# Two or four heads of a narrow causal tile in one PSUM bank: one exponential, one maximum and one mask product for them all

## The reference: one transformer block with modulation, causal attention and routed experts

```python
h = _layernorm(x) * (1 + ca) + sa
scores = jnp.einsum('bnqd,bnkd->bnqk', q, k) * HEAD_DIM ** (-0.5)
scores = jnp.where(causal, -jnp.inf, scores)          # causal: key after query
attn = jax.nn.softmax(scores, axis=-1)
out = jnp.einsum('bnqk,bnkd->bnqd', attn, v)
x = x + ga * (out @ W_out.T + b_out)
h = _layernorm(x) * (1 + cb) + sb
x = x + gb * ffn(h)      # top-4 of 16 experts per token, in 2 of 4 groups, and a shared one
```

## Time and profile before

| | |
|---|---|
| median of 3 runs | 617.59 us (617.16 to 618.82) |
| the profiled execution, its own time | 618.35 us |
| its span, first to last instruction | 616.6 us, mean granted TensorE clock 0.98 |
| busy PE, DVE, ACT, POOL | 93%, 77%, 60%, 55% of the span |
| passes 0 to 6, start to start | 32.5, 31.9, 31.8, 31.7, 37.9, 40.5, 39.6 us |
| pass 7 until its last score | 34.7 us |
| of that: exponentials L1470 | 384, 165.6 us busy |
| maxima L1586 | 384, 193.8 us busy |
| mask products L2159 | 256, 54.2 us busy |

### The profile page before, as it was taken

One profiled execution on the slowest core, in us unless ns is written; L12 is line 12 of the kernel. 1 busy time (PEld: TensorE's weight loads), 2 busy tenths in 40 slices (PEclk: granted clock), 3 DMA queues, 4 the chain that ended last, 5 costly groups with the idle time before them and its releaser, 6 DMA issues. The chain is left out here.

```text
span 616.6 us, 13827 instructions
## 1 busy us (share of the span) xinstructions
PE 570.7 (93%) x4003; PEld 386.2 (63%) x4003; DVE 472.2 (77%) x1404; ACT 372.6 (60%) x877; POOL 340.4 (55%) x646
## 2 busy tenths in 40 slices
PE   8997899999999999998987988989999999999985
PEld 7885533434343444444342466778799999999971
DVE  5868988889888769777958468898977677677647
ACT  4764566667666556655858553454566666666650
POOL 6015562656567455854648786774155655555560
PEclk9989999999999999999989879999999999999997
DMA  8489579874438281751215133567994444444895
GB/s 293 113 198 265 154 151 213 215 183 98 156 85 239 95 197 77 178 187 51 107 44 182 72 134 127 189 229 216 387 390 134 132 141 131 135 140 132 304 318 209
DMA packets 65891, 107.96 MB, mean 175 GB/s; under 512 B 13705, under 2 KB 52377, under 8 KB 64026
## 3 DMA queue, kind: packets, MB, share of 16 engines
q1 hardware_dynamic: 58954, 87.93, 49.7%
q0 software_dynamic: 6864, 19.15, 8.0%
HBM read 60.90 MB, written 43.88 MB: 170 GB/s over the span
## 5 line engine op out<-in xcount | busy, mean ns | idle before, releaser
L1470 ACT ACTIVATE Pr<-bank 128x512 f32<-128x512 f32 (+3 forms) x384 | 165.6, 495 | 97.5 <-PE bank L2276 93.5
L1586 DVE TENSOR_REDUCE mxA<-bank 128x1 f32<-128x128 f32 (+3 forms) x256 | 112.1, 483 | 20.1 <-PE bank L2161 19.7
L2276 PE MATMUL bank<-Qs,Ks 99*128 99x512 bf16 (+3 forms) x384 | 118.7, 334 | 5.0 <-ACT Pr L1470 3.2
L2161 PE MATMUL bank<-Ks,Qs 96*128 96x512 bf16 (+3 forms) x384 | 119.0, 327 | 1.2 <-DVE mxB L1586 0.6
L1292 POOL DMA_INDIRECT expert_rows<-Y,YIX x79 | 77.2, 977 | 74.2 <-ACT Y L1533 71.7
L1586 DVE TENSOR_REDUCE mxB<-bank 128x1 f32<-128x512 f32 x128 | 81.7, 681 | 13.5 <-PE bank L2161 13.5
L2262 PE MATMUL bank<-Pr,Vst 128*32 128x512 f32 (+3 forms) x768 | 83.1, 506 | 3.0 <-POOL Pr L1271 3.0
L1269 POOL TENSOR_TENSOR tick<-ident 128x1 f32<-128x1 f32 x128 | 25.3, 198 | 106.1 <-ACT Pr L1470 105.3
L2526 PE MATMUL bank<-W,xh 128*128 x316 | 78.1, 328 | 1.0 <-issue 1.0
L1221 POOL DMA_INDIRECT chosen_rows<-Hx,pos x64 | 67.2, 1049 | 20.4 <-issue 18.6
L2276 PEld LDWEIGHTS bank<-Qs,Ks 99*128 99x128 bf16 x384 | 35.9, 98 | 58.9 <-ACT Pr L1470 39.2
(11 more groups left out here) (256 smaller groups left out, 1263.6 us busy)
## 6 DMA issues: line engine op xcount, KB each, us to landing
G<-chosen_rows SPq DMA_DIRECT2D x79, 134.0 KB, 2.6
W<-expert_words SPq DMA_DIRECT2D x7, 1088.0 KB, 7.6
qk_parts<-AP SPq DMA_DIRECT2D x32, 192.0 KB, 3.1
Z<-expert_rows SPq DMA_DIRECT2D x12, 512.0 KB, 6.3
Wraw<-in_wexp SPq DMA_DIRECT2D x9, 608.0 KB, 6.4
SA<-in_wexp SPq DMA_DIRECT2D x7, 608.0 KB, 4.5
Vst<-Vall SPq DMA_DIRECT2D x8, 512.0 KB, 5.7
expert_words<-SH SPq DMA_DIRECT2D x7, 480.0 KB, 2.8
```

Of the source, the lines that this page charges most:

```text
L1470: nc.scalar.activation(Pr[(2 * s + j // 2) % 4][:, j % 2, 0:w], ebank[p % RING][:, 0:w], ACT.Exp, scale=SCALE).then_inc(exp_done, EXP)
L1586: nc.vector.tensor_reduce(dst, mbank[u % RING][:, 0:w], AX.X, ALU.max).then_inc(m_red, 1)
L2161: nc.tensor.matmul(mbank[u % RING][:, 0:w], Qs[slot][0:NPR, i // TPC, j, (i % TPC) * P:(i % TPC + 1) * P], Ks[slot][0:NPR, j, k0:k0 + w], ...
L2276: nc.tensor.matmul(ebank[p % RING][:, 0:CH - q0], Ks[slot][0:NAUG, j, kt * P:(kt + 1) * P], Qs[slot][0:NAUG, qc, j, q0:CH], start=True, st ...
```

## The change: groups instead of heads

A score tile, or unit, of width w no longer stands for one head but for n = min(4, 512 // w) heads that lie side by side in one bank: one head at 512 and 384 columns, two at 256, four at 128. Both lists (`UNIT_GROUPS`, `HEAD_GROUPS`) shrink from 48 to 38 entries a pass. A group has one exponential with an output of n rows in `Pr`, one maximum with n outputs, and one mask product whose moving operand repeats the 128 mask columns n times; its score matmuls stay one per head, and only the last of them signals. POOL's masks stay as they were, two heads at a time, but both pairs of a 128-wide step now wait for the same exponential. The rings still have three banks; the bank index now runs on over the passes, since 38 is no multiple of 3. `interleave()` places the new entries by the same rule with summed widths; the lead-in gets new counts of units per place; `UNIT_DVE` is renumbered by hand to the shorter list, and in pass 6 two routing steps follow some units. A piece of ACT's that stood after a step's second exponential now stands after the group that holds head 1.

```diff
+def packed(widths):
+    groups = []
+    for i, w in enumerate(widths):
+        n = min(HG, CH // w)
+        groups += [(i, j, n) for j in range(0, HG, n)]
+    return groups
+UNIT_GROUPS = packed([w for _, _, _, w in ROWS])
+HEAD_GROUPS = packed([step_width(_s) for _s in range(NS)])
+UNITS, HEADS = len(UNIT_GROUPS), len(HEAD_GROUPS)
...
-    unit_cost = [w + 200 for _, _, _, w in ROWS for _ in range(HG)]
-    head_cost = [CH - max(0, kt - TPC * qc) * P + EXTRA for qc, kt in STEPS for _ in range(HG)]
+    unit_cost = [n * ROWS[r][3] + 200 for r, _, n in UNIT_GROUPS]
+    head_cost = [n * step_width(i) + EXTRA for i, _, n in HEAD_GROUPS]
...
-PER_V2, PER_QK3, PER_V3 = 4, 3, 2
+PER_QK3 = 3
+AT_V2 = (0, 3, 6, 9, DIAG_UNITS)
+AT_V3 = tuple(DIAG_UNITS + 4 * KH * PER_QK3 + i for i in (0, 1, 2, 3, 3))
...
-    **{(5, 41 + t): [("aggr", 1, t)] for t in range(TPC)}, (6, 1): [("soft", 0)],
-    **{(6, 5 + i): [("route", 0, 1 + i, 2 + i)] for i in range(23)},
+UNIT_DVE.update({(6, 4): [("soft", 0)], (6, 29): [("route", 0, PLACED, PLACED + 1)], (6, 31): [("route", 0, PLACED + 1, POS_DONE)],
+                 (6, 37): [("soft", 1)]})
+for _i in range(1, PLACED):
+    _u = 5 + 17 * (_i - 1) // (SEL_DONE - 1) if _i < SEL_DONE else 22 + 6 * (_i - SEL_DONE) // (PLACED - SEL_DONE)
+    UNIT_DVE.setdefault((6, _u), []).append(("route", 0, _i, _i + 1))
...
-                        nc.scalar.activation(Pr[(2 * s + j // 2) % 4][:, j % 2, 0:w], ebank[p % RING][:, 0:w],
-                                             ACT.Exp, scale=SCALE).then_inc(exp_done, EXP)
-                        if j == 1:
+                    nc.scalar.activation(Prall[:, first:first + heads, 0:w],
+                                         ebank[(n * HEADS + p) % RING][:, 0:heads * w].rearrange("p (j w) -> p j w", w=w),
+                                         ACT.Exp, scale=SCALE).then_inc(exp_done, EXP)
+                    if j <= 1 < j + heads:
...
-                nc.vector.tensor_reduce(dst, mbank[u % RING][:, 0:w], AX.X, ALU.max).then_inc(m_red, 1)
+                nc.vector.tensor_reduce(dst, mbank[(n * UNITS + u) % RING][:, 0:heads * w].rearrange("p (j w) -> p j w", w=w),
+                                        AX.X, ALU.max).then_inc(m_red, 1)
...
-                    nc.tensor.matmul(mbank[u % RING][:, w - P:w], identb[:, :], mask[:, :], start=True, stop=False,
-                                     skip_group_check=True)
+                    nc.tensor.matmul(bank[:, :, w - P:w], identb[:, :], mask[:, :].unsqueeze(1).broadcast_to([P, heads, P]),
+                                     start=True, stop=False, skip_group_check=True)
```

More of the change, by code:

```diff
@@ L102, with step_width, group_of @@
 NS = len(STEPS)
-UNITS = len(ROWS) * HG
-HEADS = NS * HG
 EXP = 2
 RING = 3
-assert UNITS % RING == 0 and HEADS % RING == 0
+def step_width(s):
+    qc, kt = STEPS[s]
+    return CH - max(0, kt - TPC * qc) * P
+def packed(widths):
[7 more added lines that the diff above has]
+UNITS, HEADS = len(UNIT_GROUPS), len(HEAD_GROUPS)
+DIAG_UNITS = sum(1 for r, _, _ in UNIT_GROUPS if r < TPC)
 assert len(ROWS) == NS
+def group_of(groups, i, j):
+    return next(g for g, (r, first, n) in enumerate(groups) if r == i and first <= j < first + n)
 def on_diagonal(s):
@@ L141, in interleave @@
             u += 1
-            if u == HG * TPC:
+            if u == DIAG_UNITS:
                 order.append(("parts", 0))
-        if p % HG == PRODUCTS_AFTER:
+        if first + n == HG:
             order.append(("products", s - 1))
@@ L414, in program @@
             Vst[i] = att.put(f"Vst{i}", [P, KT, HG * 32], F32)
-        Pr = [att.put(f"Pr{i}", [P, 2, CH], F32) for i in range(4)]
+        Prall = att.put("Pr", [P, 2 * HG, CH], F32)
+        Pr = [Prall[:, 2 * i:2 * i + 2, :] for i in range(4)]
         outs = Area(att0 + ATT, OUTSZ)
@@ L1961, in body @@
                     max_parts(0, 0)
-                    last_v = UNITS - TPC * PER_V3
-                    for u in range(DIAG_UNITS, last_v):
+                    for u in range(DIAG_UNITS, AT_V3[0]):
                         row_maximum(0, u)
@@ L1966, in body @@
                             max_copy(0, 0, None)
-                    for v in range(2):
-                        for u in range(last_v + 2 * PER_V3 * v, last_v + 2 * PER_V3 * (v + 1)):
-                            row_maximum(0, u)
+                    for u in range(AT_V3[0], UNITS):
+                        row_maximum(0, u)
                     return
@@ L2267, in scores @@
             def scores(n, slot, turn, p):
-                s, j = p // HG, p % HG
+                s, first, heads = HEAD_GROUPS[p]
                 qc, kt = STEPS[s]
                 q0 = max(0, kt - TPC * qc) * P
-                if kt == 0 and j == 0:
+                w = CH - q0
+                if kt == 0 and first == 0:
                     pe.wait_ge(aug_in[slot][qc], turn * 48 + 48)
@@ L2275, in scores @@
                     pe.wait_ge(exp_done, n * (EXP * HEADS) + EXP * (p - RING + 1))
-                nc.tensor.matmul(ebank[p % RING][:, 0:CH - q0], Ks[slot][0:NAUG, j, kt * P:(kt + 1) * P],
-                                 Qs[slot][0:NAUG, qc, j, q0:CH], start=True, stop=True).then_inc(e_ps, 1)
+                for j in range(heads):
+                    ins = nc.tensor.matmul(ebank[(n * HEADS + p) % RING][:, j * w:(j + 1) * w],
+                                           Ks[slot][0:NAUG, first + j, kt * P:(kt + 1) * P],
+                                           Qs[slot][0:NAUG, qc, first + j, q0:CH], start=True, stop=True)
+                ins.then_inc(e_ps, 1)
             def turn_attention(c, k):
```

80 lines of the change are left out of this document (39 added, 41 removed).

## The result

The changed kernel took 611.66 us (median of 5 runs, 609.94 to 613.44), beside 617.90 for the kernel before on the same chip: ratio 0.9891, 95% interval 0.9857 to 0.9925. Its profiled execution took 611.76, with a span of 610.0. The forecast was 608.0 (604.0 to 613.5). So the direction is right and the range holds, but of 9.6 us some 6.2 came.

A forecast was written before the change was run, and what follows sets the result against it. PE sets the pace of passes 0 to 5, so its waits can be won; maxima set it in pass 6 and the lead-in. 2.0 + 0.7 + 1.4 + 1.4 + 1.0 + 0.7 + 2.4 = 9.6, giving 608.0 (604.0 to 613.5).

The forecast's parts named there:

- PE's work: Per pass 32 mask products become 22 with the same columns: 0.1 us at most, nothing booked, no loss for repeating.
- DVE's and ACT's work: Per pass, merged maxima save DVE 1.2 us; ACT's grouped exponentials are hidden by its slack in passes 0 to 6.
- Lead-in and pass 0: Together 2.0 us won: 0.8 before the first score, 0.5 up to `turn_max`, 0.7 from step 4 on.
- (A): Plain pass, first score to `turn_max`, 5.87 us in pass 2: shorter waits offset by one more 512-wide unit, net 0.
- (B): Plain pass, `turn_max` to first score of step 4: 4.48 us becomes 3.7, gain 0.75, with 0.2 in hand before the DMAs.
- Pass 1: Booked 0.7 us; nothing booked for `turn_max` to step 4, where the DMAs share queues with large transfers.
- (C): Plain pass, from step 4's first score to the end, 21.48 us: gaps of 0.95 fall to 0.25, gain 0.7.
- Pass 4: 1.0: Gain booked for pass 4, below 1.4 because the stretch from step 4 on has longer pieces between its units.
- Pass 6: Gain 2.4 us: DVE idle of 2.05 before the first routing step and 1.2 of maxima go; 0.45 and 0.6 lost, 0.2 behind.
- Pass 7 and behind: Gain 0: PE waits for DVE's unchanged chain and POOL's masks; shared expert, routing and blocks only shift.
- Half kept: Rival: DMAs a microsecond later and half the gaps after step 4 staying leave a gain of 4.9 us, 612.7; chance 0.20.
- Bigger pieces, later hand-overs: Rival: grouped units and exponentials hand over later, 3.4 us a pass, 23.5 lost if PE pays fully: 631.5; chance 0.06.

The follow-up runs named there:

- the residual early: Changed kernel with the residual's first half in passes 4 and 5 taken by DVE after unit 16 (step 5), not units 20 and 21: 609.57 us, ratio 0.9845.
- both edits: Changed kernel with the residual early and, in passes 4 and 5, ACT's late copies ahead of the merged exponential of four heads: 607.22 us, ratio 0.9843.
- Normalising first: Changed kernel with DVE normalising the pass's first output ahead of `max_parts` in passes 4 and 5: 612.24 us in its one run.
- copying first: Changed kernel with ACT's late copies of steps 3 and 11 in passes 4 and 5 ahead of the merged exponential: 609.30 us, ratio 0.9833.
- the kernel before with the entry moved: Kernel before, nothing grouped, with pass 6's first routing step behind unit 7 instead of unit 1, later ones at units 8 to 27: 616.37 us, ratio 0.9945.

## Why the prediction was right, and where it was short

*PE's work: right.* "I book nothing" for 32 mask products turned into 22, and no loss for the repeated operand: 0.22 for four heads, and no pass moves when it is undone.

*DVE's and ACT's work: right.* Four maxima in one took 0.68 with tail, as priced (0.69), the same as one over 512 columns; four exponentials in one took 0.60, as priced. From the groups of the changed kernel (busy, mean ns of one, idle before):

```profile
L1609 DVE TENSOR_REDUCE mxA<-bank 128x1 f32<-128x512 f32 x64 | 42.3, 683 | 17.0 <-PE bank L2185 17.0
L1609 DVE TENSOR_REDUCE mxA<-bank 128x4 f32<-128x512 f32 x16 | 10.9, 684 | 5.9 <-PE bank L2185 5.9
```

*Lead-in and pass 0: too small.* Forecast 2.0, measured 3.2 (1.0 before the first score, 2.2 in the pass). In (A) and (B) of pass 0, 1.4 came for the 0.5 booked. Without this error on the other side the forecast would have been further off.

*(A): a term of the sum, mis-sized by 0.25.* PE's wait before the first group's release was 0.60, not 0.4, since DVE came to that group at +1.63 and not at +1.45, and 0.15 before the next. With the unit of 0.27 that now stands there, net about +0.25 (0.18 to 0.37), not 0, in passes 1 to 5.

*(B) in plain passes: right in size, wrong in what it is worth.* 3.71 was forecast as 3.7, and the transfer did not bind in passes 2 and 3. But the step "one group has nothing to wait for", so that 0.75 is won, looked at PE and the exponentials alone. The time up to step 8 hangs on DVE, whose `max_parts` and normalisation stand in it. Pass 1 shows it: with (B) at 3.83 in one profile and 4.25 in another (the residual early, and both edits), (B) and steps 4 to 7 together took 15.87 and 15.86, and the pass 30.86 in both. In pass 2 this took back 0.19 of (B)'s 0.77. In pass 3 (B) had been 4.20 before and not 4.48 as in the pass that I had priced, so that it won 0.49. (C) gave 0.4 and 0.6 for 0.7, all of it behind step 8. Together 0.9 for 1.4, of which (A) lacks 0.25.

*(B) in passes 4 and 5: the step that failed.* The step that the forecast had wrong is that (B) there would win what it won in pass 2: "Pass 4: 1.0" took its 0.75 over. There (B) has two more pieces, and ends at a chain through ACT's copy, `max_parts` and the normalisation that is as long as before: (B) took 6.17 and 6.21 for 6.26, −0.09 and −0.05. Normalising first and copying first are worth nothing in (B) each, both together 0.5.

*The residual: priced at nothing without being looked at.* It moved from step 5 into step 6, ahead of `turn_max_waits`. The run that moves it back puts its price at 0.46 and 0.74. Together with the copy at the logits (0.67 by the run; I had booked 0.3) this is why pass 5 lost 0.8 instead of gaining 0.7.

*Pass 1: a transfer, as feared.* In the first profile (B) of pass 1 took 5.16 and ended at one of the `Qs<-MT` DMAs:

```profile
116.49 0.39 PE L2303 MATMUL bank<-Qs,Ks 99*128 99x512 bf16 x1 [1.21 <-DMA Qs<-MT]
```

In the other profiles of versions with everything shared it took 3.83 to 4.56 (6.38 at the clock of 0.95), before 4.64, and 4.20 in the kernel before with the entry moved. It varies from one execution to the next, with the pass 30.86 when it lands in time: −1.0 then, −0.1 in the profiled one. So 0.6 of what the forecast lacked in the profiled execution is this.

*Pass 6: right in size, in part by luck.* 2.4 for 2.4, but 0.4 of the measured 2.4 is the clock in the last 7 us of this pass in the kernel before; at one clock it is 2.0. The term of 2.05 is seen: the kernel before with the entry moved wins 2.0 up to `turn_max`. But there 1.1 of it comes back behind, and the changed kernel wins 1.1 more than that one, where the other terms of the sum came to 0.35. The parts are off both ways.

*Pass 7 and behind: right.* The 1.3 won up to its last score (at a granted clock of 0.95 for 0.92) is mostly lost to the wait for POOL, and at the last product 0.3 is left. What stands behind it took 256.5 for 257.6; nothing here shows why.

*The rivals.* "Half kept" described the size (4.9, measured 6.2) but not the cause: the DMAs kept 0.6 of the forecast in pass 1 and nothing in passes 2 to 5, and the masks kept nothing. "Bigger pieces, later hand-overs", with the Trainium skill's rule (Perfetto Trace Analysis, Optimizing Scalar/DVE Operations) that breaking up instructions may let work finish sooner, would have given 631.5. The changed kernel's traces show its kind of wait only in (A), and there it cost 0.25 a pass. The version near 626, with shared scores alone, comes closest to it, as its last unit has to stand behind four scores in one piece; but the maxima that PE waits for there are the small ones, and they start late instead of taking longer.

## What to carry to other kernels

When an edit changes how many units a pass has, every table keyed by unit numbers moves work: price each entry by the wait that stands next behind its new place, on the engine that waits, not by its own length. A wait that ends with one engine's work may have a second right behind it, so that removing either alone gives nothing; follow the chain to the piece that starts it. And a gain read at one wait of the pacing engine counts only up to the next place where another engine, which has no slack in that stretch, is waited for.
